# A four-layer graph network on one core: three scalings moved to another engine, a broadcast by DRAM in place of matmuls, and two steps moved

## What is computed

```python
# layer 0: A' = a*A with (1-a) added on the diagonal
x = relu(((1/rowsum(A'))[:, None] * A' @ h) @ W.T + b)
# layer 1, for two heads i: graph attention, mask = adj > 0
e = leaky_relu(s_src[:, None] + s_dst[None, :]);  att = softmax(where(mask, e, NEG)) @ hh + x
h_next += elu(layernorm(att) @ ff1_w[i].T) / 2        # hh = layernorm(x) @ ff0_w[i].T
# layer 2: one attention head, slope 0.2, relu(att @ Wh)
# layer 3: (H.T @ X) / H.sum(axis=0)[:, None], H = adj
```

## Time and profile before

| | |
|---|---|
| median of 3 runs | 1193.92 us (1193.82 to 1194.11) |
| the profiled execution | 1193.39 us, of which 1191.6 us are the span from the first to the last instruction |
| granted TensorE clock | 1.0 throughout |
| TensorE busy | 1185.7 us |
| VectorE busy | 938.3 us |
| ScalarE busy | 325.5 us |
| layer 0, the last quarter ends | 246.87 us |
| code's h = 1 / h = 3 begin | 246.87 / 728.1 us |

### The profile page before, as it was taken

How to read it: one execution, slowest core, us unless ns; L and a number is a source line. 1 busy time by engine, 2 the same in 40 slices (tenths; PEclk the granted TensorE clock), 3 DMA queues, 4 the chain that set the end, 5 groups by cost and what they waited for, 6 DMA issues and landing times.

```text
span 1191.6 us, 16721 instructions
## 1 busy us (share of the span) xinstructions
PE 1185.7 (100%) x6235; PEld 816.7 (69%) x6235; DVE 938.3 (79%) x1677; ACT 325.5 (27%) x780; POOL 9.6 (1%) x20
## 2 busy tenths in 40 slices
PE   9999999999999999999999999999999999999999
PEld 9999999954444444444454547999999964444455
DVE  5548585798979787889797787788787869887786
ACT  4512122225323242423445234541212121000000
POOL 3000000000000000000000000000000000000000
DMA  9888898800111102110010101032303068999920
GB/s 324 304 279 291 248 347 305 282 29 15 40 18 37 18 35 35 53 18 22 1 22 0 40 1 40 1 108 90 141 0 141 1 268 304 313 329 322 322 82 18
DMA packets 90227, 156.30 MB, mean 131 GB/s; under 512 B 45904, under 2 KB 54448, under 8 KB 90160
## 3 DMA queue, kind: packets, MB, share of 16 engines
q1 hardware_dynamic: 64240, 148.58, 36.3%
q10 hardware_dynamic: 25456, 6.30, 2.4%
q0 software_dynamic: 464, 0.53, 0.2%
HBM read 146.94 MB, written 4.78 MB: 127 GB/s over the span
## 4 chain that ended last, share of the span: by engine, by line
PE 94%; DVE 4%; ACT 1%; DMA 0%; issue 0%; DVEq 0%; ACTq 0%
PE acc L555 48%; PE acc L539 36%; PE acc L802 4%; DVE ring L1367 2%; PE mix L621 1%; PE mix L593 1%; PE mix L608 1%; PE acc L810 1%; PE turn L570 1%; DMA ring<-in_adj_t 0%; DVE G L1367 0%; PE mix L670 0%; ACT V L829 0%; DVE stats L1170 0%; ACT U L829 0%
## 5 line engine op out<-in xcount | busy, mean ns | idle before, releaser
L1367 DVE SCALAR_TENSOR_TENSOR ring<-G,score,mask 128x1024 f32<-128x1024 f32 x372 | 466.8, 1280 | 70.9 <-PE acc L555 38.7
L555 PE MATMUL acc<-ring,G 128*128 128x512 f32 x1000 | 436.3, 593 | 0.3 <-DVE acc L1305 0.2
L555 PEld LDWEIGHTS acc<-ring,G 128*128 128x128 f32 x1000 | 186.5, 190 | 229.6 <-issue 210.9
L539 PE MATMUL acc<-G,ring 128*128 128x129 f32 x2240 | 253.9, 275 | 0.8 <-DVE acc L1316 0.7
L539 PEld LDWEIGHTS acc<-G,ring 128*128 128x128 f32 x2240 | 251.9, 192 | 2.1 <-DVE ring L1367 2.0
L539 PE MATMUL acc<-G,mask 128*128 128x129 f32 x1648 | 185.8, 275 | 0.0
L539 PEld LDWEIGHTS acc<-G,mask 128*128 128x128 f32 x1648 | 184.8, 192 | 0.0
L555 PE MATMUL acc<-mask,G 128*128 128x512 f32 x384 | 165.8, 593 | 0.0
L1637 DVE TENSOR_TENSOR ring<-ring,mask 128x1024 f32<-128x1024 f32 x120 | 146.8, 1223 | 11.0 <-DVE ring L1637 0.5
L555 PEld LDWEIGHTS acc<-mask,G 128*128 128x128 f32 x384 | 72.6, 190 | 91.0 <-issue 89.8
L1405 DVE TENSOR_SCALAR mask<-mask 128x1024 uint8<-128x1024 f32 x103 | 68.4, 689 | 27.4 <-DMA mask<-in_adj_t 26.8
(11 more groups left out here) (207 smaller groups left out, 707.0 us busy)
## 6 DMA issues: line engine op xcount, KB each, us to landing
mask<-in_adj SPq DMA_DIRECT2D x128, 512.0 KB, 5.5
mask<-in_adj_t SPq DMA_DIRECT2D x103, 512.0 KB, 5.2
ring<-in_adj_t SPq DMA_DIRECT2D x18, 512.0 KB, 6.4
G<-given_rows SPq DMA_DIRECT2D x10, 512.0 KB, 3.9
G<-in_adj_t SPq DMA_DIRECT2D x4, 512.0 KB, 6.4
G<-raw_rows SPq DMA_DIRECT2D x4, 512.0 KB, 5.2
inputs<-V ACTq DMA_DIRECT2D x4, 512.0 KB, 2.7
V<-inputs SPq DMA_DIRECT2D x4, 512.0 KB, 3.9
```

Of the source, the lines that this page charges most:

```text
L539: mm = pe.matmul(acc[:, b, (s % 3) * DW:(s % 3) * DW + DW], lhs[:, s * P:(s + 1) * P], g, start=(k == 0 and s % 3 == 0), stop=(k == T - 1) ...
L555: mm = pe.matmul(acc[:, c, :], g, moving[:, c * BANK:(c + 1) * BANK], start=(k == 0), stop=(k == T - 1), skip_group_check=True)
L1367: dve.scalar_tensor_tensor(slots[k % L], late_home[h] if early and k >= EARLY else rows_home[h, q], rank[h][:, k:k + 1], span(mask, (q * T ...
```

## The change

1. The four vectors for the dots no longer go through TensorE and PSUM. SyncE writes `qcol` (128 x 4, single elements of 4 bytes at a stride) to a DRAM row behind the issue of tile 15 of quarter 1, issues tiles 16 and 17, waits for that write, and loads the row back, broadcast over the partitions, in two DMAs (64 KB and 192 KB). VectorE's hook behind mask 9 waits for both instead of copying.
2. Parts 0 and 1 of layer 1's G are scaled by ScalarE, behind `early_exponentials(1)` and ahead of `post0(Q - 1)`; part 3 too, in `late_rows(1)` between the late row exponential and the fold's copies. VectorE does none of them. ScalarE scales 8 tiles in 8 instructions.
3. The late copy of layer 1's raw row is issued behind tile 31 of layer 0's last quarter.
4. In layer 3's first quarter VectorE's `scal` moves from behind product 8 to behind product 7 (ahead of product 8), and the two steps of the late maximum from behind product 22 to behind product 23.

```diff
+        dot_rows = nc.dram_tensor("dot_rows", (4 * P,), F32, kind="Internal").ap()
...
-            layer0(1)
+            layer0(1, range(T // 2))
+            sp.wait_ge(back_placed, 1)
+            sp.dma_start(dot_rows.rearrange("(c p) -> p c", p=P), qcol, allow_slow_non_contiguous=True).then_inc(dots_written, 16)
+            layer0(1, range(T // 2, T // 2 + 2))
+            sp.wait_ge(dots_written, 16)
+            sp.dma_start(w0T, dot_rows[0:P].partition_broadcast(P)).then_inc(dots_loaded, 16)
+            sp.dma_start(spare[:, o:o + 3 * D], dot_rows[P:4 * P].partition_broadcast(P)).then_inc(dots_loaded, 16)
+            layer0(1, range(T // 2 + 2, T))
...
-            layer0(3, range(2 * S + 2, 3 * S + 2))
+            layer0(3, range(2 * S + 2, T))
             sp.wait_ge(slot_used, (Q - 1) * (T - 1) + 2 * S)
             load_raw(1, late_home[1])
-            layer0(3, range(3 * S + 2, T))
...
-            def spread_dots():
-                pe.wait_ge(back_placed, 1)
-                for c in range(4):
-                    mm = spread(qcol[:, c:c + 1], mix[:, 0, c * P:(c + 1) * P])
-                mm.then_inc(dots_spread, 1)
-            run(0, 1, {3: turn_weights_back, 6: spread_dots})
+            run(0, 1, {3: turn_weights_back})
...
                 row_exponentials(h, late_home[h], kept_rows[h])
                 if h == 1:
+                    scale_g(1, Q - 1)
                     act.wait_ge(fold_spread, 1)
...
-                act.wait_ge(v_made, early_top[h])
+                act.wait_ge(v_made, late_top[h] if part == Q - 1 else early_top[h])
...
             early_exponentials(1)
+            scale_g(1, 0)
+            scale_g(1, 1)
...
-            def keep_dots():
-                dve.wait_ge(dots_spread, 1)
-                dve.tensor_copy(w0T, mix[:, 0, 0:P])
-                dve.tensor_copy(spare[:, o:o + 3 * D], mix[:, 0, P:4 * P]).then_inc(dots_kept, 1)
-                dve.wait_ge(dots_kept, 1)
+            def dots_there():
+                dve.wait_ge(dots_loaded, 32)
...
-            stage0(1, {4: place_back, 9: keep_dots})
+            stage0(1, {4: place_back, 9: dots_there})
             quarters(dve, 2, Q - 2, stage0, st, STAGE0)
             early = early_of(1)
-            stage0(Q - 1, {21: early[0], 24: early[1], 30: lambda: scale_g(1, 0), 31: lambda: scale_g(1, 1)})
+            stage0(Q - 1, {21: early[0], 24: early[1]})
...
-                return [lambda: (first(), second()), lambda: scale_g(h, Q - 1), lambda: scale_sums(h)]
+                return [lambda: (first(), second())] + ([] if h == 1 else [lambda: scale_g(h, Q - 1)]) + [lambda: scale_sums(h)]
...
-            ks = [4, 4, 6, 8, 8, 11, 11, 14, 15, 16, 22, 23, 25, 26, 27, 30]
+            ks = [4, 4, 6, 8, 8, 11, 11, 14, 15, 16, 22, 25, 26, 27, 30]
...
-            ks = [3,4,5,7,8,14,14,14,16,17,21,22,23,24,25,27]
+            ks = [3, 4, 5, 7, 7, 14, 14, 14, 16, 17, 21, 23, 23, 24, 25, 27]
```

More of the change, by code:

```diff
@@ L210, in graph_layers @@
         h_turned, h_wide, h_projected, h_placed = sem("h_turned"), sem("h_wide"), sem("h_projected"), sem("h_placed")
-        dots_spread, dots_kept = sem("dots_spread"), sem("dots_kept")
+        dots_written, dots_loaded = sem("dots_written"), sem("dots_loaded")
         f_turned, f_wide, f_projected, f_placed = sem("f_turned"), sem("f_wide"), sem("f_projected"), sem("f_placed")
```

## The result

The changed kernel takes **1197.86 us** (median of 7 runs, 1196.88 to 1199.48) where the kernel before took 1194.11 beside it (7 runs): a ratio of **1.0039, 95% interval 1.0029 to 1.0048**. It is slower by 3.7 us; 1190.2 was forecast. (The two medians alone give 1.0031, inside that interval.) Its runs also lie 2.6 us apart, those of before 1.6.

A forecast was written before the change was run, and what follows sets the result against it. TensorE bounds the kernel, busy 1185.7 of 1191.6 us. Terms 0.44 + 1.76 + 0.59 + 1.12 - 0.2 = 3.7 us take its execution from 1193.4 to 1189.7, median 1190.2; 8-in-10 range 1189.4 to 1192.6.

The forecast's parts named there:

- (a): Layer 0, second quarter: four spreads leave TensorE, 0.44 us off the path; the two VectorE copies worth nothing.
- (b): Layer 1, first quarter: two G scalings leave VectorE, its products start earlier; gain 1.76 us, bounds 1.5 and 1.8.
- The alternative bound of 1.5: Lower bound of layer 1's scalings gain, if half of VectorE's chain meets a ScalarE step that didn't move.
- (c): Layer 1's last G part scaled by ScalarE ahead of the fold's copies, margin 0.1 us: zero, bounds 0 and 0.3 lost.
- (d): Layer 3, first quarter: scales step ahead of product 8, turn of V on time; gain 0.59 us, bounds 0.4 and 0.65.
- (e): Layer 3, first quarter: product 23 ahead of the maximum's step, tile 24 earlier; gain 1.12 us, bounds 0.9 and 1.35.
- (f): Late raw row issued behind layer 0's last tiles, which land sooner and help VectorE begin layer 1: zero by itself.
- (g): Round trip through DRAM, layer 0's second quarter: loads land at 99.7, likeliest loss 0.2 us, bounds 0 and 5.8.
- The sign that was named for being wrong: TensorE showing idle time between 105 and 132 us waiting for tiles; no size given.
- the deadline: Layer 0, second quarter: the round trip's loads must land by 100.4 (99.8 with 4.6) or TensorE waits for tile 21.
- the round trip that makes it slower: Rival, chance 0.05: write takes 10.4, loads land at 113.3, stall 12.9, 1203 us; decides from a stall above 6.3.
- The Trainium skill's rule: Fixed DMA cost of about 2 us plus bytes: the small write would land at 91.6, the round trip costing nothing, 1190.0.

The follow-up runs named there:

- no round trip: Changed kernel with the round trip taken back (four spreads on TensorE, two copies on VectorE): 1191.09 us, ratio 0.9984 against the kernel before.
- wait behind mask 16: Changed kernel with VectorE's wait for the loads behind mask 16 instead of mask 9: 1190.51 us, ratio 0.9977 against the kernel before.
- the probes' traces (5 and 6): Two kernels: wait behind mask 16 plus extra small DRAM writes near 400 us, varying element number or distance; whole time not counted, up to the four-column product 82.22 and 81.93.
- experiment 5: Wait behind mask 16 plus five small writes in a quiet stretch: 512, 256, 128 elements landed in 8.7, 8.6, 7.8 us; 512 spaced by 64 bytes in 2.5.
- experiment 10: Wait behind mask 16, with the late raw row back between tiles 25 and 26 of layer 0's last quarter: 1191.46 us, ratio 0.9991 against the kernel before.
- experiment 7: Changed kernel with the small write behind tile 12 and loads behind tile 14, VectorE's wait still behind mask 9: 1192.46 us, ratio 0.9991 against the kernel before.

## Why the prediction was wrong, step by step

- **(a) Spreads off TensorE, 0.44.** Right as a price: the second stretch is 165.14 with them and 164.72 without (no round trip against wait behind mask 16). It was kept in that trace alone: in the probes' traces (5 and 6) the late tile 18 took it back, 165.12 and 165.10.
- **(b) Scalings off VectorE, 1.76.** Right in kind, 1.76 where 1.0 was found on average, three quarters too large. I read the stall from a single execution, and it varies with the last tile's landing; and I let VectorE start at 241.6 "if the last tile has landed". In that very trace it landed at 241.7, its mask takes 0.7 more, and the first of the two scalings stood in the wait for it. The alternative bound of 1.5 was still too high.
- **(c) The last part on ScalarE, zero.** Right. The scaling ended at 294.54 + 2.44 = 296.98 and the copies waited another 0.20 for TensorE; a margin of 0.1 was expected. Tile 24 comes 14.44 behind the turn in both kernels (293.98 - 279.54, 299.13 - 284.69).
- **(d) and (e), layer 3, 0.59 and 1.12.** Right: 0.60 and 1.12, and the tile-to-tile distances of 14.3 and about 7.5 that were to show it.
- **(f) The raw row.** No effect on the lead in the one trace with the row back, so nothing shows that it helped (b) begin, as I wrote. On the time, open.
- **(g) The round trip, 0.2.** This is the step that failed, and in it one term: the write. I had the row of the same kind of transfer, 10.4 us for 1024 elements, and took "halfway for half the elements", 5.9. It took 9.1 to 10.2 in every kernel that has it in this form, because what costs is not the number (experiment 5). That is 3.2 of the delay. The loads took 6.1 from the write's landing where 4.2 stood (0.8 for the issues and 3.4, the row of a 64 KB load, while the later one here has 192 KB): 1.9. The write was issued 0.4 late. So the loads landed at 105.1 in place of 99.7. The sign that was named for being wrong, TensorE waiting for tiles between 105 and 132 us, is there. Nothing was gained by the finer working of the deadline (100.4) when the estimate for the landing was 0.7 below it, and its other end 5.8 above.
- **The deadline** itself held for the second quarter: 105.1 is 4.4 behind it, allowing 0.3 for the later start, and tile 19 was 4.24 late in all; the rest of the quarter added 1.0, half of it in tile 19, where TensorE started anew at its lower clock. It was too kind further on, since I took a queue that runs dry to be quick, and didn't follow the bunch of tiles into the third quarter, where it meets the raw row's write. That added 1.6 in the changed kernel, and 0.9 and 1.7 us in kernels whose second quarter was unharmed (165.61 and 166.42 against 164.72). In experiment 10 it was 1.3 without a bunch.
- **The rivals.** The one that came true by its result is the round trip that makes it slower, with a chance of 0.05. 6.9 were lost (171.59 - 165.15 + 0.44), above the 6.3 from which it decided. Of its mechanism the slow write was right (9.1, not 10.4), but the loads did not land as late as the slowest tile: they came at 105.1, short of the 106.7 that it asked for, and the second quarter alone lost 5.3. What carried the loss over 6.3 was the third quarter, which no rival had. A term whose range reached 5.8 should have had a wider share of the forecast.
- The Trainium skill's rule of a fixed cost of about 2 us ("DMA: Bandwidth & Descriptors", "Anatomy of one DMA"), which that section gives for DMAs that GpSimd issues, is near what the writes in runs of 16 bytes or at distances from 16 bytes took here from SyncE (1.4 to 3.2 us) and not the ones side by side (7.5 to 8.7).

## What to carry to other kernels

Put a wait on a DMA in an engine's queue just ahead of the first use of the data, and count what stands behind it: here one number, hook 9 or hook 16, decided between 3.7 us lost and 2.9 gained. Where a term's nearest row is far away, take the row's own value as the likely one until something shows how it scales. A stall read from one execution may be as long as another execution's landing lets it be; what hangs on a landing was worth less here than it showed (1.0 of 1.76), and what hangs on an order of instructions just that (0.60 and 1.12). Work that fills a wait cost nothing here: taking the first of the two scalings away only uncovered the wait.

## What the runs showed of the hardware

Writes of single 4-byte elements to DRAM that lie side by side land in 7.5 to 8.7 us in a quiet queue, for 128 elements as for 512; at 16 bytes of distance 1.7, at 32 1.4, at 64 3.2, and in runs of 16 bytes 1.4. The tiles issued next to such a write land later: 8.3 us in the kernel before for the tile next to the raw row's write, where its predecessor took 4.7, and 13.1 in experiment 7.

TensorE's clock fell behind the stall of the changed kernel. The windows (from:to, us; then busy time and count of TensorE, weight load, VectorE, ScalarE, GpSimd, the granted clock, DMA share, GB/s):

```profile
108.00:110.00 2.00, 0.12 (x1) 0.13 (x2) 0.24 (x2) 1.73 (x5) 0.00 (x0) 1.00 0.91 311
110.00:112.00 2.00, 2.00 (x13) 2.00 (x14) 1.93 (x14) 0.00 (x0) 0.00 (x0) 0.66 0.76 254
112.00:114.00 2.00, 1.78 (x8) 1.49 (x8) 1.90 (x9) 0.21 (x1) 0.00 (x0) 0.50 0.43 143
114.00:116.00 2.00, 2.00 (x20) 2.00 (x19) 1.94 (x4) 1.73 (x5) 0.00 (x0) 0.98 0.83 209
```

After 2.46 us without work, up to 109.88, the engine ran at 0.50, its level of 1.2 GHz, and tile 18's products took 3.12 us in place of 1.95. The kernel with the round trip alone kept 1.00 behind waits of 1.66 and 1.31 us, at 109.26 and 116.70. Behind one of 1.95 us, in the third quarter, its clock fell too:

```profile
153.41 44.79 PE L547 MATMUL acc<-G,mask 128*128 128x129 f32 x384 [1.95 <-DMA mask<-in_adj_t]
```
```profile
152.00:154.00 2.00, 0.59 (x5) 0.59 (x6) 0.61 (x2) 0.00 (x0) 0.00 (x0) 0.98 0.96 295
154.00:156.00 2.00, 2.00 (x12) 2.00 (x11) 1.90 (x13) 0.17 (x1) 0.00 (x0) 0.50 1.08 360
156.00:158.00 2.00, 2.00 (x14) 2.00 (x14) 1.93 (x7) 0.41 (x3) 0.00 (x0) 0.67 1.06 396
```

There it had a price. The 384 products took 44.79 us, where the same 384 of the changed kernel, at full clock, took 43.15: 1.6 us. The kernel lost 173.12 - 165.15 + 0.44 = 8.4 us in all, and 6.8 without this, against 6.9 in the changed kernel. In the changed kernel the slow clock cost little, but that is argued from the rows, not shown by a run. Tile 18's slow products had ended when tile 19 landed (0.21 us of the time before 113.21 was a wait for it). Tile 19's products ran at 0.50 until about 114, an estimated 0.4 us longer (half of 0.8), and TensorE had to wait again for tiles 23 and 25, which hides some of that.
